# Latent attention: softmax sums by GpSimd and per chunk, two VectorE jobs on ScalarE, maximum read before the copy

## The chip, the cores and the metric

The kernel runs on one NeuronCore of a Trainium2 chip. The metric is the device time of one execution in microseconds (us), and lower is better. TensorE does matrix products into PSUM; VectorE and ScalarE read and write PSUM and SBUF; GpSimd works on SBUF alone. Each engine runs its own instructions in the order of the program and meets the others at semaphores.

## The reference

Two transformer-like layers on x of 2048 tokens by 256. The change touches only the first attention (16 heads, causal, queries and keys of 128 + 64 columns through low-rank latents):

```
q = (_rmsnorm(x @ w_q_a, q_a_ln) @ w_q_b).reshape(b, s, H, DQ)
q_nope, q_pe = (q[..., :DN], q[..., DN:])
ckv = x @ w_kv_a
c_kv, k_pe = (ckv[..., :KL], ckv[..., KL:])
kv = (_rmsnorm(c_kv, kv_a_ln) @ w_kv_b).reshape(b, s, H, DN + DV)
q_pe = _apply_rope(q_pe, cos, sin)
...
scores = jnp.einsum('bqhd,bkhd->bhqk', qf, kf) * scale
scores = jnp.where(mask[None, None], scores, jnp.finfo(scores.dtype).min)
p = jax.nn.softmax(scores, axis=-1)
o = jnp.einsum('bhqk,bkhd->bqhd', p, v).reshape(b, s, H * DV)
return o @ w_out
```

Before it stands a routed FFN; after it a second routed FFN, a mixing FFN, a second attention and another mixing FFN. None of these is touched.

## The kernel before

`latent_heads` does the first attention. Heads go in 8 pairs, and the 2048 queries in 4 chunks of 512 (`CH`), j = 0 to 3. A unit is one head of one chunk, so there are 64 units; the two units of a pair and a chunk stand one behind the other and share a chunk's end (32 of those). Keys go in tiles of 128, and a step is two key tiles: unit j has 2(j+1) steps, the last two of them on the diagonal (tiles of 512, 384, 256 and 128 queries), 320 steps in all. Scores are kept with keys on the partitions and queries along the row.

A step goes through these events:
- `scores`: per key tile three products (high and low parts of query and key) into one of two score buffers in PSUM, used in turn;
- `evac`: ScalarE copies the tile to a slot of `held` in SBUF; `max`: VectorE takes the running maximum per key partition from the same PSUM buffer into `largest`. A score buffer is free for step n + 2 once both are done;
- after the unit's last `max`: `turn_max` (four transposes), `turn_max_out` (VectorE: row maxima, then a diagonal matrix of their negatives, `shift_diag`, L1237 and L1242), `spread` (one product that puts the shift on all partitions);
- some 12 steps behind its scores (`SECOND_PASS_AFTER`): `add` (VectorE adds the shift), `exp` (ScalarE), `values` (TensorE, two 64-column products side by side), and `sum` (GpSimd adds the exponentials of the full tiles into `summed`, L1178 and L1182; diagonal tiles get none);
- per unit `sums` (L1027, L1029): TensorE multiplies `summed` and each diagonal tile, loaded as weights, by one column of ones, 28 instructions for j > 0 and 20 for j = 0; `sums_out` takes the reciprocals (L1283);
- per chunk `widen`, `spread_inverse`, `project`: scaling, and the output projection added to x (L1295).

Each unit's query is made ahead of its scores: `query` (five products), `query_out` (ScalarE copy, L1124), `sine` (VectorE, two 32-partition multiplications with halves exchanged, L1260 and L1261), `cosine`, `whole` (GpSimd, L1188 and L1192), `high` (ScalarE), `low` (GpSimd, L1197).

The order of events on each engine is fixed before the program runs by `latent_plan`: every event has an engine, an estimated duration, a rank and the events it must follow, and a list scheduler walks through them. `HELD_STEPS` (15) is the number of slots of `held`; `evac` of step n waits until step n - 15 has been multiplied and summed. Products outside the score path (`SIDE`) share two PSUM banks in turn.

## Time and profile before

| | us |
|---|---|
| median of 3 runs | 2220.66 |
| lowest, highest | 2203.05, 2222.22 |
| the profiled execution, time | 2205.07 |
| its span, first to last instruction | 2203.3 |
| first attention's heads (`latent_heads`) in it | 146 to 1472, so 1326 |

Over the span TensorE is busy 91%, VectorE 75%, ScalarE 51% and GpSimd 36%, at a mean granted TensorE clock of 0.883. These shares mix stages with different limits. The page of the profile and the trace give times in us, of single instructions in ns; PE is TensorE, PEld its weight loads, DVE VectorE, ACT ScalarE, POOL GpSimd. L1029 is line 1029 of the kernel. The granted clock is a share of full speed, 1.00 for 2.4 GHz and 0.50 for 1.2 GHz. Busy matmuls overlap in the records, so the distance from start to start is the better price of one.

### The profile page before, as it was taken

How to read it: one execution, taken by the hardware profiler on the slowest of the kernel's cores; microseconds unless marked ns; L12 is line 12 of the kernel's file. 1: busy time of each engine (PE TensorE's matmuls, PEld its weight loads, DVE VectorE, ACT ScalarE, POOL GpSimd, SP SyncE). 2: the span in 40 equal slices, each digit the busy share in tenths (PEclk: the TensorE clock that was granted, in tenths of full speed). 3: DMA queues.
4: the chain of work that ended last, by engine and by line, in shares of the span. 5: the costliest groups of instructions: out<-in, count | busy, mean ns of one | idle time of the engine just before them, and what ended most of it. 6: DMA issues, size and time to landing. Idle time of an engine off the chain costs nothing. (4 is left out here: it accounts for less than half of the span.)

```text
span 2203.3 us, 30217 instructions
## 1 busy us (share of the span) xinstructions
PE 2000.7 (91%) x10904; PEld 1238.1 (56%) x10904; DVE 1660.8 (75%) x2525; ACT 1114.9 (51%) x2075; POOL 792.0 (36%) x636
## 2 busy tenths in 40 slices
PE   4769999999999999999999999957497899999996
PEld 3646656657657657566666666636454444444436
DVE  6758887786887796787786887756856788888725
ACT  1235664564564564564564555521032457777771
POOL 0015564563664572573573663430231100000010
PEclk8878998998898998898998898967798779999998
DMA  2200000000000000000000000010233020020001
GB/s 89 69 21 1 1 1 13 1 1 6 8 1 6 9 1 13 1 1 14 1 1 5 1 1 1 1 41 1 71 68 70 2 30 1 1 30 2 2 1 39
DMA packets 26707, 34.53 MB, mean 16 GB/s; under 512 B 5312, under 2 KB 19648, under 8 KB 26432
## 3 DMA queue, kind: packets, MB, share of 16 engines
q1 hardware_dynamic: 25360, 31.28, 6.0%
q8 instruction: 89, 1.46, 0.3%
q10 hardware_dynamic: 1200, 1.31, 0.2%
q14 instruction: 58, 0.48, 0.1%
HBM read 26.03 MB, written 6.29 MB: 15 GB/s over the span
## 5 line engine op out<-in xcount | busy, mean ns | idle before, releaser
L1100 ACT ACTIVATE lath_held<-lath_score 128x512 f32<-128x512 f32 (+1 forms) x448 | 293.5, 686 | 321.3 <-PE lath_score L993 318.7
L1182 POOL TENSOR_TENSOR lath_summed<-lath_summed,lath_held 128x512 f32<-128x512 f32 x288 | 387.5, 1345 | 130.3 <-ACT lath_held L1105 111.7
L1251 DVE TENSOR_TENSOR lath_held<-lath_held,lath_shift 128x512 f32<-128x512 f32 (+1 forms) x448 | 339.5, 792 | 50.5 <-PE lath_shift L1016 49.2
L1895 ACT ACTIVATE atth_probs<-atth_score 128x512 f32<-128x512 f32 (+3 forms) x640 | 293.2, 541 | 153.4 <-PE atth_score L1814 151.1
L1105 ACT ACTIVATE lath_held<-lath_held 128x512 f32<-128x512 f32 (+1 forms) x448 | 306.8, 719 | 116.9 <-DVE lath_held L1251 115.2
L1004 PE MATMUL lath_out<-lath_held,lat_latent 128*64 128x512 f32 (+3 forms) x1280 | 342.3, 599 | 2.4 <-ACT lath_held L1105 2.4
L1854 DVE TENSOR_REDUCE atth_maxima<-atth_slot 128x2 f32<-128x1024 f32 (+3 forms) x288 | 286.0, 1042 | 54.3 <-PE atth_slot L1797 53.3
L989 PE MATMUL lath_score<-lath_query_hi,lat_key_hi 128*128 128x512 f32 (+3 forms) x640 | 281.4, 440 | 10.2 <-DVE lath_largest L1205 7.1
L993 PE MATMUL lath_score<-lath_query_hi,lat_key_lo 128*128 128x512 f32 (+3 forms) x640 | 271.8, 425 | 0.0
L1205 DVE TENSOR_TENSOR lath_largest<-lath_score,lath_largest 128x256 f32<-128x256 f32 (+3 forms) x336 | 222.2, 685 | 62.0 <-ACT lath_held L1100 58.6
L990 PE MATMUL lath_score<-lath_query_lo,lat_key_hi 128*128 128x512 f32 (+3 forms) x640 | 252.4, 394 | 0.0
L989 PEld LDWEIGHTS lath_score<-lath_query_hi,lat_key_hi 128*128 128x128 f32 x640 | 133.6, 209 | 182.1 <-issue 123.7
L1742 POOL TENSOR_SCALAR_AFFINE_SELECT atth_probs<-atth_probs 128x512 f32<-128x512 f32 x64 | 40.8, 637 | 430.8 <-ACT atth_probs L1895 430.8
L1029 PE MATMUL lath_side<-square,lath_held 128*128 128x1 f32 x1280 | 184.1, 260 | 0.5 <-ACT lath_held L1105 0.5
L1029 PEld LDWEIGHTS lath_side<-square,lath_held 128*128 128x128 f32 x1280 | 174.0, 206 | 4.7 <-issue 3.0
L1178 POOL TENSOR_TENSOR lath_summed<-lath_held 128x512 f32<-128x512 f32 x48 | 62.3, 1298 | 307.5 <-ACT lath_held L1105 294.7
L1188 POOL TENSOR_TENSOR lath_turn_a<-lath_query,lat_rope 128x512 f32<-128x512 f32 x64 | 95.5, 1492 | 199.2 <-ACT lath_query L1124 197.8
L1827 PE MATMUL atth_out<-atth_probs,att_v_one 128*32 128x512 f32 (+3 forms) x1280 | 152.1, 549 | 0.6 <-POOL atth_probs L1742 0.5
L993 PEld LDWEIGHTS lath_score<-lath_query_hi,lat_key_lo 128*128 128x128 f32 x640 | 137.6, 215 | 19.9
L990 PEld LDWEIGHTS lath_score<-lath_query_lo,lat_key_hi 128*128 128x128 f32 x640 | 135.4, 212 | 15.8
L1004 PEld LDWEIGHTS lath_out<-lath_held,lat_latent 128*64 128x64 f32 x1280 | 70.4, 144 | 94.0 <-issue 71.6
L1814 PE MATMUL atth_score<-atth_query,att_key 50*128 50x512 f32 (+3 forms) x384 | 116.1, 453 | 1.7 <-ACT atth_probs L1895 1.1
(342 smaller groups left out, 3098.4 us busy)
## 6 DMA issues: line engine op xcount, KB each, us to landing
att_first_query<-att_scratch SPq DMA_DIRECT2D x12, 256.0 KB, 9.0
atth_query<-att_scratch SPq DMA_DIRECT2D x12, 256.0 KB, 8.9
ffn_a_w<-in_L_ffn_W SPq DMA_DIRECT2D x2, 1024.0 KB
lat_raw_out<-in_L_attn_w_out SPq DMA_DIRECT2D x8, 256.0 KB, 2.7
lat_rope<-in_c_rope_feature SPq DMA_DIRECT2D x1, 2048.0 KB, 11.0
ffn_b_w<-in_L_ffn_W SPq DMA_DIRECT2D x2, 1024.0 KB, 7.1
mix_a_factors<-in_L_ffn_factors SPq DMA_DIRECT2D x8, 256.0 KB, 4.0
att_scratch<-attp_high SPq DMA_DIRECT2D x4, 512.0 KB, 2.9
```

Source lines behind the costliest of these rows:

```text
L989: nc.tensor.matmul(scores[:, q0:CH], key_hi[:, keys], hi, start=True, stop=False)
L990: nc.tensor.matmul(scores[:, q0:CH], key_hi[:, keys], lo, start=False, stop=False)
L993: last = nc.tensor.matmul(scores[:, q0:CH], key_lo[:, keys], hi, start=False, stop=True)
L1004: last = nc.tensor.matmul(out_bank[KL * i:KL * i + KL, q0:CH], latent[:, kt, 0:KL], slot(n)[:, i, q0:CH], start=(step == 0), stop=(step == ...
L1029: last = nc.tensor.matmul(bank[:, i:i + 1], slot(end - 2 + d // 2)[:, d % 2, cols], core.ones[:, 0:1], start=(j == 0 and d == 0), stop=(d ...
L1100: nc.scalar.activation(slot(n)[:, tiles, q0:CH], score_bank[n % 2][:, tiles, q0:CH], ACT.Copy)\
L1105: nc.scalar.activation(slot(n)[:, tiles, q0:CH], slot(n)[:, tiles, q0:CH], ACT.Exp, scale=SCALE0)\
L1182: nc.gpsimd.tensor_tensor(total, total, slot(n)[:, i, :], ALU.add).then_inc(s["tiles_summed"], 1)
L1205: nc.vector.tensor_tensor(out, first, second, ALU.max).then_inc(s["maxed"], 1)
L1251: nc.vector.tensor_tensor(slot(n)[:, tiles, q0:CH], slot(n)[:, tiles, q0:CH], shift[:, q0:CH].unsqueeze(1).broadcast_to([P, count, CH - q0 ...
L1854: nc.vector.reduce_max(maxima[:, n % 2, :, pair, i, at], slot[r % 2][:, :, begin:begin + width], AX.X)\
L1895: nc.scalar.activation(probs[:, step % PROB_STEPS, h, q0:CH], score_bank[u % 3][:, q0:CH], ACT.Exp, scale=SCALE1)\
```

## The change

- `sum` now covers the diagonal tiles too: GpSimd adds all four at their own widths (512, 384, 256, 128 queries), for j = 0 as well, beginning there with a zero. `summed` has four buffers in place of two.
- `sums` is done once per chunk. Two products with ones as weights (64 columns each, one head in each half of the bank) give the sums along the row; `sums_out` copies them to SBUF (ScalarE), `turn_sums` turns them with four transposes, and `turn_sums_out` takes all reciprocals at once (VectorE).
- `shift_diag` is made by ScalarE in four copies with a scale per partition (`diag`), no longer by VectorE.
- ScalarE exchanges the halves of the rotated query columns while it copies them from PSUM (two more copies in `query_out`), and VectorE multiplies once on 64 partitions. The sign in the table moves with it.
- `max` waits for the scores alone (at step 1 of a unit for the copy of step 0 too), and `evac` waits for `max`. The scores of step n + 2 wait for `evac` alone.
- `HELD_STEPS` is 14, and the estimates in the plan follow the new work.

```diff
-HELD_STEPS = 15
+HELD_STEPS = 14
@@ sum_parts
-    return 0 if s >= 2 * j else 1 if s == 0 else 2
+    return 1 if s == 0 and LATENT_UNITS[u][1] else 2
@@ tensor
                             pe.wait_ge(s["evacuated"], PARTS_DONE[n - 2])
-                            if MAX_DONE[n - 2]:
-                                pe.wait_ge(s["maxed"], MAX_DONE[n - 2])
...
                     elif kind == "sums":
-                        for i in range(TPC):
-                            cols = slice(i * P, (i + 1) * P)
-                            if j:
-                                nc.tensor.matmul(bank[:, i:i + 1], summed[:, n % 2, cols], core.ones[:, 0:1], start=True, stop=False)
-                            for d in range(i + 1):
-                                last = nc.tensor.matmul(bank[:, i:i + 1], slot(end - 2 + d // 2)[:, d % 2, cols], core.ones[:, 0:1],
-                                                        start=(j == 0 and d == 0), stop=(d == i))
+                        pe.wait_ge(s["tiles_summed"], SUMS_DONE[FIRST_STEP[2 * n + 2] - 1])
+                        for h in range(2):
+                            last = nc.tensor.matmul(bank[KL * h:KL * h + KL, :], core.ones[:, 0:KL], summed[:, (2 * n + h) % 4, :], start=True, stop=True)
+                        last.then_inc(s["side_done"], 1)
+                    elif kind == "turn_sums":
+                        pe.wait_ge(freed(("sums", n)), use["sums", n] // 2 + 1)
                         for i in range(TPC):
+                            last = nc.tensor.transpose(bank[:, i * P:(i + 1) * P], sums_t[:, i * P:(i + 1) * P], core.ident)
@@ scalar
                     if kind == "evac":
                         act.wait_ge(s["scores_done"], n + 1)
+                        if max_parts(n):
+                            act.wait_ge(s["maxed"], MAX_DONE[n] - (1 if j and step == 2 * j + 1 else 0))
...
+                    elif kind == "diag":
+                        act.wait_ge(freed(("turn_max", n)), use["turn_max", n] // 2 + 1)
+                        if n:
+                            act.wait_ge(s["spread_done"], n)
+                        for i in range(TPC):
+                            nc.scalar.activation(shift_diag[:, i], minus_ident[:], ACT.Copy, scale=row_max[:, n % 2, i:i + 1]).then_inc(s["diag_ready"], 1)
+                    elif kind == "sums_out":
+                        wait_side(act, ("sums", n))
+                        nc.scalar.activation(sums_t[:], side(("sums", n))[:], ACT.Copy).then_inc(freed(("sums", n)), 1)
...
                         whole = side(("query", n))
+                        nc.scalar.activation(turn_b[64:96], whole[96:P], ACT.Copy).then_inc(s["halves_swapped"], 1)
+                        nc.scalar.activation(turn_b[96:P], whole[64:96], ACT.Copy).then_inc(s["halves_swapped"], 1)
@@ gpsimd
                         for i in range(2):
+                            q0 = queries_from(2 * step + i, j)
+                            so_far = total[:, q0:CH]
+                            if step == 0 and i == 0:
+                                so_far = zero[:].broadcast_to([P, CH])
+                            else:
+                                pool.wait_ge(s["tiles_summed"], before + i)
+                            nc.gpsimd.tensor_tensor(total[:, q0:CH], so_far, slot(n)[:, i, q0:CH], ALU.add).then_inc(s["tiles_summed"], 1)
@@ vector
                     if kind == "max":
-                        dve.wait_ge(s["evacuated"], PARTS_DONE[n])
+                        dve.wait_ge(s["scores_done"], n + 1)
+                        if step == 1 and j:
+                            dve.wait_ge(s["evacuated"], PARTS_DONE[n - 1])
...
-                        nc.vector.tensor_tensor(shift_diag[:], minus_ident[:].unsqueeze(1).broadcast_to([P, TPC, P]),
-                                                row_max[:].unsqueeze(2).broadcast_to([P, TPC, P]), ALU.mult).then_inc(s["diag_ready"], 1)
...
-                        nc.vector.tensor_tensor(turn_b[64:96], query[96:P, n % 2], rope[96:P, 1, cols], ALU.mult).then_inc(s["sine_done"], 1)
-                        nc.vector.tensor_tensor(turn_b[96:P], query[64:96, n % 2], rope[64:96, 1, cols], ALU.mult).then_inc(s["sine_done"], 1)
+                        dve.wait_ge(s["halves_swapped"], 2 * n + 2)
+                        nc.vector.tensor_tensor(turn_b[64:P], turn_b[64:P], rope[64:P, 1, cols], ALU.mult).then_inc(s["sine_done"], 1)
```

The first place is TensorE at the end of a unit halfway through the stage (the second head of chunk 2 of pair 3, where a chunk ends as well). `lath_score` is a score buffer, `lath_side` a side bank. Before:

```order
L993 MATMUL lath_score0<-lath_query_hi,lat_key_lo 128x512
L1027 MATMUL lath_side0<-square,lath_summed 128x1
L1029 MATMUL lath_side0<-square,lath_held 128x1
L1027 MATMUL lath_side0<-square,lath_summed 128x1
L1029 MATMUL lath_side0<-square,lath_held 128x1 x2
L1027 MATMUL lath_side0<-square,lath_summed 128x1
L1029 MATMUL lath_side0<-square,lath_held 128x1 x3
L1027 MATMUL lath_side0<-square,lath_summed 128x1
L1029 MATMUL lath_side0<-square,lath_held 128x1 x4
L1010 MATMUL lath_side1<-square,lath_largest 128x128 x4
L1004 MATMUL lath_out<-lath_held,lat_latent 64x512 x2
```

and now, at the same chunk's end:

```order
L987 MATMUL lath_score0<-lath_query_hi,lat_key_lo 128x512
L1015 MATMUL lath_side1<-lath_summed,square 64x512 x2
L1004 MATMUL lath_side0<-square,lath_largest 128x128 x4
L998 MATMUL lath_out<-lath_held,lat_latent 64x512 x2
L1020 MATMUL lath_side1<-square,lath_sums_t 128x128 x4
L983 MATMUL lath_score1<-lath_query_hi,lat_key_hi 128x512
```

The 14 one-column products of the unit (each is two instructions in the trace) are gone; the other unit of the chunk has none at all now, and this one has two wide products and four transposes.

The second place is GpSimd over the sums of the first head of chunk 3 of the same pair. Before:

```order
L1178 TENSOR_TENSOR lath_summed<-lath_held 128x512
L1182 TENSOR_TENSOR lath_summed<-lath_summed,lath_held 128x512 x4
L1188 TENSOR_TENSOR lath_turn_a<-lath_query,lat_rope 128x512
L1182 TENSOR_TENSOR lath_summed<-lath_summed,lath_held 128x512 x6
L1197 TENSOR_TENSOR lath_query_lo<-lath_query,lath_query_hi 128x512
```

and now:

```order
L1183 TENSOR_TENSOR lath_summed<-lath_held 128x512
L1192 TENSOR_TENSOR lath_summed<-lath_summed,lath_held 128x512 x4
L1198 TENSOR_TENSOR lath_turn_a<-lath_query,lat_rope 128x512
L1192 TENSOR_TENSOR lath_summed<-lath_summed,lath_held 128x512 x4
L1202 TENSOR_TENSOR lath_query<-lath_turn_a,lath_turn_b 128x512
L1207 TENSOR_TENSOR lath_query_lo<-lath_query,lath_query_hi 128x512
L1192 TENSOR_TENSOR lath_summed<-lath_summed,lath_held 128x512 x3
L1192 TENSOR_TENSOR lath_summed<-lath_summed,lath_held 128x384
L1192 TENSOR_TENSOR lath_summed<-lath_summed,lath_held 128x256
L1192 TENSOR_TENSOR lath_summed<-lath_summed,lath_held 128x128
```

The unit's sum now ends with its four diagonal tiles, and the jobs of the next queries stand between them and behind them.

## Rows read from the trace of the kernel before

**Rows 1.** Windows view, the stage: us; busy PE, PEld, DVE, ACT, POOL; granted clock; DMA share.

```profile
146.00:1472.00 1326.00, 1289.14 (x6297) 831.17 (x6296) 1031.37 (x1408) 727.48 (x1216) 711.67 (x528) 0.89 0.02 5
```

**Rows 2.** Groups by line and form, TensorE: the sums' one-column products.

```profile
L1029 PE MATMUL lath_side<-square,lath_held 128*128 128x1 f32 x1280 | 184.1, 260 | 0.5 <-ACT lath_held L1105 0.5
...
L1027 PE MATMUL lath_side<-square,lath_summed 128*128 128x1 f32 x384 | 68.6, 248 | 10.6 <-POOL lath_summed L1182 7.6 <-DVE x L1295 1.6 <-ACT lath_held L1105 1.4
```

**Rows 3.** Timeline, TensorE: start us, us, instructions merged.

```profile
1085.81 1.03 PE L1004 MATMUL lath_out<-lath_held,lat_latent 128*64 128x512 f32 x4
...
1086.76 0.50 PE L989 MATMUL lath_score<-lath_query_hi,lat_key_hi 128*128 128x512 f32 x1
...
1088.26 0.28 PE L1027 MATMUL lath_side<-square,lath_summed 128*128 128x1 f32 x2
...
1090.41 1.03 PE L1029 MATMUL lath_side<-square,lath_held 128*128 128x1 f32 x8
...
1091.31 0.63 PE L1010 MATMUL lath_side<-square,lath_largest 128*128 128x128 f32 x4
...
1145.54 0.66 PE L1010 MATMUL lath_side<-square,lath_largest 128*128 128x128 f32 x4
```

**Rows 4.** Windows view, TensorE: us, busy (count), granted clock, DMA share, GB/s.

```profile
1090.00:1092.00 2.00, 2.00 (x19) 1.00 0.00 0
...
1092.00:1094.00 2.00, 2.00 (x6) 0.62 0.00 0
...
1096.00:1098.00 2.00, 2.00 (x9) 1.00 0.00 0
...
1147.00:1150.00 3.00, 3.00 (x16) 1.00 0.00 0
```

**Rows 5.** Waits, TensorE: score products (total us, times, longest).

```profile
PE lath_score L989 <- DVE lath_largest L1205: 7.1, 13, 1.1
```

**Rows 6.** Groups by line and form, GpSimd.

```profile
L1182 POOL TENSOR_TENSOR lath_summed<-lath_summed,lath_held 128x512 f32<-128x512 f32 x288 | 387.5, 1345 | 130.3 <-ACT lath_held L1105 111.7
...
L1197 POOL TENSOR_TENSOR lath_query_lo<-lath_query,lath_query_hi 128x512 fp32r<-128x512 f32 x64 | 89.7, 1402 | 54.3 <-ACT lath_query_hi L1129 54.3
...
L1192 POOL TENSOR_TENSOR lath_query<-lath_turn_a,lath_turn_b 128x512 f32<-128x512 f32 x64 | 82.2, 1284 | 54.2 <-DVE lath_turn_b L1261 53.2 <-PE lath_side L1029 0.7
...
L1588 POOL TENSOR_TENSOR attp_turned<-attp_by_cos,attp_by_sin 128x256 f32<-128x256 f32 x16 | 13.6, 848 | 50.4 <-DVE attp_by_sin L1563 50.4
```

**Rows 7.** Groups by line and form, VectorE.

```profile
L1261 DVE TENSOR_TENSOR lath_turn_b<-lath_query,lat_rope 32x512 f32<-32x512 f32 x64 | 78.8, 1232 | 2.0
...
L1260 DVE TENSOR_TENSOR lath_turn_b<-lath_query,lat_rope 32x512 f32<-32x512 f32 x64 | 71.4, 1115 | 10.4 <-ACT lath_query L1124 7.0 <-POOL lath_query L1192 1.5
...
L1205 DVE TENSOR_TENSOR lath_largest<-lath_score,lath_largest 128x1024 f32<-128x1024 f32 x96 | 117.1, 1219 | 30.7 <-ACT lath_held L1100 29.9
...
L1242 DVE TENSOR_TENSOR lath_shift_diag<-lath_minus_ident,lath_row_max 128x512 fp32r<-128x512 f32 x64 | 55.3, 865 | 2.2
```

**Rows 8.** Timeline, VectorE and GpSimd: a sine pair.

```profile
1304.77 0.69 DVE L1260 TENSOR_TENSOR lath_turn_b<-lath_query,lat_rope 32x512 f32<-32x512 f32 x1
...
1305.48 1.66 DVE L1261 TENSOR_TENSOR lath_turn_b<-lath_query,lat_rope 32x512 f32<-32x512 f32 x1
...
1304.78 1.81 POOL L1197 TENSOR_TENSOR lath_query_lo<-lath_query,lath_query_hi 128x512 fp32r<-128x512 f32 x1
```

**Rows 9.** Groups by line and form, ScalarE.

```profile
L1100 ACT ACTIVATE lath_held<-lath_score 128x1024 f32<-128x1024 f32 x192 | 196.0, 1021 | 198.3 <-PE lath_score L993 196.3
...
L1113 ACT ACTIVATE lath_half<-lath_out 64x512 f32<-64x512 f32 x48 | 28.6, 596 | 19.8 <-PE lath_out L1004 18.9
...
L1105 ACT ACTIVATE lath_held<-lath_held 128x128 f32<-128x128 f32 x64 | 19.4, 303 | 0.0
```

**Rows 10.** Timeline, the stage's end: last GpSimd sums, last residual add.

```profile
1444.07 13.67 POOL L1182 TENSOR_TENSOR lath_summed<-lath_summed,lath_held 128x512 f32<-128x512 f32 x10
...
1470.77 0.69 DVE L1295 TENSOR_TENSOR x<-lath_side,x 128x512 f32<-128x512 f32 x1 [1.01 <-PE lath_side L1044]
```

More of the change, by code:

```diff
@@ L732 @@
 PER_PAIR = 2 * NCH
-HELD_STEPS = 15
+HELD_STEPS = 14
 SECOND_PASS_AFTER = 12.0
 QUERY_SLOTS = 3
-SIDE = ("turn_q", "turn_kv", "fold_query", "fold_out", "query", "turn_max", "sums", "spread_inverse", "project")
+SIDE = ("turn_q", "turn_kv", "fold_query", "fold_out", "query", "turn_max", "sums", "turn_sums", "spread_inverse", "project")
 def step_parts(g):
@@ L810, in latent_plan @@
         k, due, last = NCH * p + j, FIRST_STEP[u] - 6.0, FIRST_STEP[u + 1] - 1
-        add("tensor", 1.3, due, ("query", u), ("split_low", p), of("low", u - 2))
-        add("scalar", 0.55, due, ("query_out", u), ("query", u))
-        add("vector", 1.2, due, ("sine", u), ("query_out", u), of("whole", u - 1))
+        add("tensor", 1.3, due, ("query", u), ("split_low", p), of("low", u - 2), of("whole", u - 1))
+        add("scalar", 1.5, due, ("query_out", u), ("query", u))
+        add("vector", 0.9, due, ("sine", u), ("query_out", u))
         add("pool", 1.3, due, ("cosine", u), ("query_out", u), of("whole", u - 1))
@@ L838, in latent_plan @@
         held = g - HELD_STEPS
-        add("tensor", 0.1 + 3 * total / 2250, g, ("scores", g), ("low", u), of("scores", g - 1), of("evac", g - 2), of("max", g - 2))
-        full = s < 2 * j
-        if held < 0:
-            summed = None
-        elif LATENT_STEPS[held][1] < 2 * LATENT_UNITS[LATENT_STEPS[held][0]][1]:
-            summed = ("sum", held)
-        else:
-            summed = ("sums", LATENT_STEPS[held][0])
-        add("scalar", on_scalar, g, ("evac", g), ("scores", g), of("values", held), summed)
-        add("vector", 0.0 if j and s == 0 else elementwise + (0.6 if j and s == 2 * j + 1 else 0.0), g + 1.0, ("max", g), ("evac", g),
-            of("max", g - 1), of("turn_max", u - 2) if s == 0 else None)
-        add("vector", elementwise, late - 1.0, ("add", g), ("spread", u), ("max", g), of("add", g - 1))
+        add("tensor", 0.1 + 3 * total / 2250, g, ("scores", g), ("low", u), of("scores", g - 1), of("evac", g - 2))
+        add("scalar", on_scalar, g, ("evac", g), ("max", g), of("values", held), of("sum", held))
+        add("vector", 0.0 if j and s == 0 else elementwise + (0.6 if j and s == 2 * j + 1 else 0.0), g, ("max", g), ("scores", g), of("evac", g - 1), of("max", g - 1),
+             of("turn_max", u - 2) if s == 0 else None)
+        add("vector", elementwise, late - 1.0, ("add", g), ("spread", u), ("evac", g), of("add", g - 1))
         add("scalar", on_scalar, late - 0.6, ("exp", g), ("add", g), of("exp", g - 1))
@@ L853, in latent_plan @@
             of("fold", u - 1) if s == 0 else None)
-        if full:
-            add("pool", sum_parts(g) * 1.3, late, ("sum", g), ("exp", g), ("sum", g - 1) if s else None, of("sums", u - 2) if s == 0 else None)
+        add("pool", (1.3 if sum_parts(g) == 1 else sum(0.15 + w / 420 for w in widths) if len(widths) > 1 else 2.6), late, ("sum", g), ("exp", g), of("sum", g - 1),
+            of("sums", u // 2 - 2) if s == 0 else None)
     followers, missing = {}, {}
@@ L1114, in _ @@
                     elif kind == "widen":
-                        for u in (2 * n, 2 * n + 1):
-                            act.wait_ge(freed(("sums", u)), use["sums", u] // 2 + 1)
+                        act.wait_ge(freed(("turn_sums", n)), use["turn_sums", n] // 2 + 1)
                         if n:
@@ L1172, in _ @@
                         _, j, _ = LATENT_UNITS[u]
[L1173 removed]
+                        total, before = summed[:, u % 4], SUMS_DONE[n] - sum_parts(n)
                         pool.wait_ge(s["exp_done"], PARTS_DONE[n])
[L1175 to L1177 removed]
+                        if step == 0 and u >= 4:
+                            wait_side(pool, ("sums", u // 2 - 2))
+                        if step == 0 and j:
                             nc.gpsimd.tensor_tensor(total, slot(n)[:, 0, :], slot(n)[:, 1, :], ALU.add).then_inc(s["tiles_summed"], 1)
```

77 lines of the change are left out of this document (35 added, 42 removed).

## The prediction

> **What bounds the kernel now.** I read the windows view first, since the change touches one stage only. From 146 to 1472 us, 1326 us of the span, TensorE is busy 1289, VectorE 1031, ScalarE 727 and GpSimd 712 [rows 1]. So TensorE sets the pace of this stage and every other engine has slack. The waits confirm it: over 320 steps the score products waited 7.1 us for VectorE's maximum [rows 5]. What TensorE spends its time on is the groups view, and there the one-column products for the softmax sums stand out: 1280 and 384 instructions, 184.1 and 68.6 us busy, for results four columns wide [rows 2]. The timeline gives their real price, since busy times overlap: the 28 instructions of one unit begin at 1088.26 and the next work at 1091.31, so 3.05 us, or 0.109 us each [rows 3]. The third view is the granted clock. It stands at 1.00 (2.4 GHz) while such a run goes by, falls to 0.62 of full speed on average in the window behind it (part of it at 0.50, 1.2 GHz), and is back at 1.00 by 1096 [rows 4]. What TensorE did right before the fall was this run of one-column products. Over the stage the mean is 0.89 [rows 1].
>
> **The change, part by part.** Everything is a sum against the profiled execution, 2205.07 us, with the stage's 1326 us as the part that moves.
>
> *Sums on TensorE.* The 1664 one-column instructions go: 1664 x 0.109 = 181 us at the full clock. New are, per chunk, two products of 512 columns in the two halves of a bank, in form like a step of `values`, which took 0.95 us from 1085.81 to the next start at 1086.76, and four transposes like `turn_max`, 0.63 us [rows 3]. 32 x 1.58 = 51 us. Net -130.
>
> *The clock.* A mean of 0.89 between two levels of 0.5 and 1 says that 22% of the stage, 292 us, ran at 1.2 GHz. If the cause is the one-column runs and they are gone, the same work takes 146 us less. That is the other half of the gain, and it takes no cover from anywhere: -146. Bounds: nothing if another cause cools the clock, -146 if none does. I take the whole, because the rows beside a lone `turn_max` (1145.54, four transposes as in the new code) show the window after it at 1.00 [rows 3, 4]. TensorE's own floor for the stage is then 1326 - 130 - 146 = 1050 us.
>
> *Sums on GpSimd.* It gets four more additions per unit, 1280 columns. In proportion to the 512-column addition of 1.345 us that is 3.36 us; the 256-column row with 0.848 us says that short ones cost more than their share, and a straight line through the two gives 0.35 us each plus the columns, 3.88 us [rows 6]. 64 units: 215 to 248, I take 232. GpSimd's work becomes 712 + 232 = 944 us. It is no longer the idle engine, and its queue has waits that more slack doesn't remove: 54.3 us for ScalarE's high part and 54.2 us for VectorE's sine, with the query chain of three jobs going to and fro [rows 6]. I keep both, 108. At the start of the stage it has nothing for about 9 us plus some 15 us of ramp before exponentials exist (an estimate), and behind its last sum at 1457.7 the stage goes on for 14 us to 1471.5 [rows 10]. 944 + 108 + 24 + 14 = 1090 us. **GpSimd becomes the bound**, 40 us above TensorE.
>
> *VectorE.* `shift_diag` goes (55.3), the two sine jobs of 1.12 and 1.23 us become one [rows 7]. The new one has the same number of columns on 64 partitions; an undisturbed one took 0.69 and one beside a GpSimd job 1.66 [rows 8], so 44 to 106 us against 150 before; I take 75. VectorE: 1031 - 55 - 75 = about 900 us (870 to 932), off the bound.
>
> *ScalarE.* Four 128-column copies per unit, by the 303 ns row 78 us; two half copies from PSUM per query, 128 at the 0.596 us of a copy of 64 partitions, 76 us; 32 copies of sums, 19 us [rows 9]. 727 + 173 = 900 us, off the bound, with a longer queue.
>
> *Order of maximum and copy.* The score buffer is freed by the same two jobs in the other sequence: 1.22 (maximum) and 1.02 (copy) [rows 7, 9]. No gain on that chain: 0 by itself. What it moves is who waits: ScalarE's copy now stands in its queue until VectorE is done, and behind it are exponentials (for which TensorE's values and GpSimd's sums wait), query copies and the new diagonal copies. Cover: exponentials run some steps ahead of the values that need them. If the cover fails it costs TensorE a part of a step each time; that is the second rival. One slot of `held` less tightens the same loop, since a copy waits for the sum of 14 steps before: 12 steps of lag leave GpSimd two steps, some 5 us, to be late in.
>
> *Tail and constants.* The last unit's four extra additions, 3.4 to 3.9 us, stand behind 13.67 us of its sums [rows 10]; the shorter product run behind them gives about that back. One more memset and a sign in a table: nothing.
>
> **The sum.** GpSimd's 1090, plus 20 us for slips, since TensorE stood idle 37 us in the stage even when it alone was short [rows 1] and four engines will now be at 80% or more. Stage 1110, so 216 us less: 2205 - 216 = 1989. The profiled execution was 15.6 us below the median of the runs shown; the scatter between 2203 and 2222 is most likely the machine's, and I give the new kernel two thirds of it: **2000 us**.
>
> *Where the skill speaks against it.* GpSimd and VectorE get in each other's way in this trace: at 1304.77 a sine job ran its 0.69 us while the GpSimd job that began with it took 1.81, against its group's mean of 1.40, and the next sine job took 1.66 [rows 6, 8]. The Trainium skill, GPSIMD Engine Reference, Specifications, says that GpSimd's SBUF interfaces are shared with VectorE, with contention when VectorE has two SBUF inputs; by that rule, the trace agrees, a fuller GpSimd meets more such jobs. But the change also takes away one sine job and the diagonal per unit, 128 of 240 such jobs. Were every one of the 112 that remain to cost GpSimd those 0.4 us, it would be 45 us on its 1090, within the second rival.
>
> **Rivals.**
>
> *TensorE keeps the pace.* GpSimd's 108 us of waits were slack that closes when it is busy, its sums slide past them, and the stage ends near TensorE's 1050 to 1070: 2205 - 266 + 11 = 1950. For it: the waits of rows 6 were measured on an idle engine. Against it: four engines at 85 to 95%.
>
> *Lockstep.* All four engines wait for each other a little in queues of fixed order, because the estimates by which the order was laid down differ from the true durations (in the plan GpSimd's low part stands at 1.3 us and ScalarE's wide copy at 0.95, against 1.40 and 1.02 measured [rows 6, 9]). Taken as 0.25 to 0.5 us of new TensorE wait per step, 320 steps give 80 to 160 us over the floor of 1050, to which new idle time might add a colder clock: stage 1150 to 1230, 2040 to 2120. For it: the balance above. Against it: before, with VectorE at 78%, TensorE lost almost nothing.
>
> *The clock still falls.* If transposes and idle time cool it as the one-column products did, each chunk's new pair and four transposes next to `turn_max` bring one cold stretch as long as one behind each of the 64 runs before, 292 / 64 = 4.6 us, half of it lost: 32 x 2.3 = 74 us on top, about 2075. Against it: the window behind the lone transposes [rows 4]. The Trainium skill, TensorE: Matmul & The Clock Gate, Part 4, says that transposes don't count as busy for the clock gate; by that rule this rival would come true, and the lone `turn_max` speaks against it here.
>
> *Slower.* The place is the score buffer. For two steps the loop is one set of scores (1.50 us [rows 3]), maximum 1.22, copy 1.02 and some 0.6 us of hand-overs, 4.3 us, against TensorE's own 2 x 2.45 = 4.9 us at full clock. It fits with 0.6 us to spare. If at each turn a shift addition (1.2) stands ahead of the maximum and an exponential (1.05) ahead of the copy, the loop is 6.6 us and TensorE waits 0.85 us per step; 320 x 0.86 = 276 us eats the whole gain, and from there on the kernel is slower; with a clock that cools in those waits, about 2250. For it: ScalarE's queue is now behind VectorE's. Against it: the same two jobs in the other sequence were in this loop before, and TensorE waited 7.1 us in all [rows 5].
>
> **How the numbers follow.** GpSimd's pace 0.52 (1975 to 2030), TensorE's pace 0.13 (1935 to 1975), lockstep 0.25 (2030 to 2120), clock 0.04 (2050 to 2090), slower 0.04, no change within 1% 0.02. The range leaves out the lower end of the TensorE case and the upper ends of lockstep and slower: 1942 to 2105. A measurement of this kernel can tell about 1% from no change. Faster by over 1%: 0.94; within: 0.02; slower: 0.04.
>
> **What would show it.** In the profile after: a granted clock of 0.97 or more over the stage, with no fall behind the chunk sums (the clock term); GpSimd busy 930 to 960 us there and rarely idle except in the query chain; TensorE busy below 95% of the stage, its waits naming ScalarE's copies or, at the chunk's sums, GpSimd; VectorE and ScalarE each near 900 us. Wrong would be: a mean clock at 0.9 still; short GpSimd additions well over 1 us each; score products that wait for the copy through the whole of chunk 3; or GpSimd's waits shrinking to a few us, which leaves TensorE's pace and a time under 1960.

## The result, and the profile after

The changed kernel takes 2015.72 us (median; 2009.53 to 2020.40) against 2220.65 us (2203.05 to 2222.22), a ratio of 0.9086 with a 95% interval of 0.9039 to 0.9133. Its profiled execution took 2015.19 us.

The windows view of the first attention's stage, with the columns of [rows 1] (us; busy PE, PEld, DVE, ACT, POOL; granted clock; DMA share):

```profile
141.00:1267.00 1126.00, 1053.63 (x4896) 611.67 (x4896) 886.50 (x1254) 883.67 (x1633) 923.52 (x784) 0.97 0.02 5
```

The stage has gone from 1329 us (142 to 1471; the 1326 of [rows 1] begin 4 us later) to 1126. TensorE is busy 1054 us, 235 less than in [rows 1], and its clock is 0.97 in place of 0.89. GpSimd has 924 us, VectorE 887, ScalarE 884. Of these 203 us the execution keeps some 190: from the stage's end to the end of the span it is 746 us now and was 732, in code that the change doesn't touch (experiment 8 comes back to this).

What answers to [rows 2] is one group of 128 instructions (count, busy us and mean ns, idle before) in place of 1664:

```profile
L1015 PE MATMUL lath_side<-lath_summed,square 128*64 128x512 f32 x128 | 38.7, 663 | 19.3 <-POOL lath_summed L1192 18.2 <-ACT lath_query L1129 0.9
```

On TensorE's timeline a chunk's end looks like this, as [rows 3] did for a unit's:

```profile
902.09 1.08 PE L1015 MATMUL lath_side<-lath_summed,square 128*64 128x512 f32 x4
...
902.97 1.08 PE L998 MATMUL lath_out<-lath_held,lat_latent 128*64 128x512 f32 x4
...
903.98 0.66 PE L1020 MATMUL lath_side<-square,lath_sums_t 128*128 128x128 f32 x4
...
904.39 0.48 PE L983 MATMUL lath_score<-lath_query_hi,lat_key_hi 128*128 128x512 f32 x1
```

The pair of wide products takes 0.88 us to the next start (902.09 to 902.97), the four transposes 0.41 (903.98 to 904.39). And against [rows 4] the clock now falls nowhere behind the sums of a chunk. Inside the stage it falls at the start of a pair of heads, six times; the rest of its time at 1.2 GHz stands in the stage's first 40 us and in its tail. One of the six (windows of 4 us, TensorE busy, granted clock):

```profile
728.00:732.00 4.00, 1.94 (x11) 1.00 0.00 0
...
732.00:736.00 4.00, 3.08 (x8) 0.64 0.01 2
...
736.00:740.00 4.00, 4.00 (x13) 0.51 0.00 0
...
740.00:744.00 4.00, 4.00 (x23) 1.00 0.00 0
```

TensorE was busy for 1.94 of 4 us with the clock at 1.00, and then it is 0.64 and 0.51. Here it stood idle before the fall, and in the 4 us before each of the other five it was busy for 1.73 to 2.04 us. Before the change it fell right behind one-column products with TensorE busy all the time: of its 52 falls between 170 and 1440 us, 51 have such products in the 4 us ahead of them. TensorE's waits (total us, times, longest), beside [rows 5]:

```profile
PE lath_score L983 <- ACT lath_held L1090: 21.2, 31, 1.7
...
PE lath_side L1015 <- POOL lath_summed L1192: 18.2, 10, 10.6
...
PE lath_out L998 <- ACT lath_held L1095: 5.6, 4, 3.0
```

They are short and of several kinds. Together with the rest the stage has 72 us in which TensorE is idle, 37 before.

GpSimd's groups, beside [rows 6]:

```profile
L1192 POOL TENSOR_TENSOR lath_summed<-lath_summed,lath_held 128x512 f32<-128x512 f32 x336 | 443.7, 1321 | 31.3 <-ACT lath_held L1095 6.6 <-POOL lath_summed L1183 0.4
...
L1192 POOL TENSOR_TENSOR lath_summed<-lath_summed,lath_held 128x256 f32<-128x256 f32 x64 | 49.7, 776 | 5.2
...
L1192 POOL TENSOR_TENSOR lath_summed<-lath_summed,lath_held 128x128 f32<-128x128 f32 x64 | 32.7, 511 | 5.0
...
L1207 POOL TENSOR_TENSOR lath_query_lo<-lath_query,lath_query_hi 128x512 fp32r<-128x512 f32 x64 | 84.7, 1323 | 9.3 <-ACT lath_query_hi L1134 9.3
...
L1202 POOL TENSOR_TENSOR lath_query<-lath_turn_a,lath_turn_b 128x512 f32<-128x512 f32 x64 | 84.8, 1325 | 4.7 <-DVE lath_turn_b L1269 3.5
```

The 512-column addition costs what it did. The short ones, 776 and 511 ns, are dearer than their share of columns. And the two waits of the query chain, 54.3 and 54.2 us before, are 9.3 and 4.7. GpSimd's largest wait in the stage is another, for the exponentials at a unit's first sum:

```profile
POOL lath_summed L1183 <- ACT lath_held L1095: 89.8, 23, 8.5
```

The new sine job of VectorE and the new copies of ScalarE, beside [rows 7, 9]:

```profile
L1269 DVE TENSOR_TENSOR lath_turn_b<-lath_turn_b,lat_rope 64x512 f32<-64x512 f32 x64 | 65.8, 1028 | 30.6 <-ACT lath_turn_b L1128 21.7 <-PE lath_score L987 7.7
```

```profile
L1102 ACT ACTIVATE lath_shift_diag<-lath_minus_ident,lath_row_max 128x128 fp32r<-128x128 f32 x256 | 81.6, 393 | 19.5 <-DVE lath_row_max L1252 19.2
...
L1127 ACT ACTIVATE lath_turn_b<-lath_side 32x512 f32<-32x512 f32 x64 | 37.8, 591 | 16.7 <-PE lath_side L1043 15.5
```

At the stage's end, beside [rows 10]:

```profile
1240.07 16.17 POOL L1192 TENSOR_TENSOR lath_summed<-lath_summed,lath_held 128x512 f32<-128x512 f32 x13
...
1256.38 1.98 PE L1015 MATMUL lath_side<-lath_summed,square 128*64 128x512 f32 x4 [10.58 <-POOL lath_summed L1192]
...
1266.98 0.69 DVE L1303 TENSOR_TENSOR x<-lath_side,x 128x512 f32<-128x512 f32 x1 [1.02 <-PE lath_side L1034]
```

GpSimd's last sums run for 16.17 us and end at 1256.24; only then can TensorE start the last chunk's products, and the stage ends 11.4 us later.

### The profile page after: what moved, and what is told of

It is laid out like the page before. It is cut to its first block and busy times, and to the rows that moved or that the text cites. A ratio compares the mean times of both kernels' runs of the same rounds, so it can differ in the third digit from the quotient of the medians.

```text
span 2013.2 us, 28359 instructions
## 1 busy us (share of the span) xinstructions
PE 1776.6 (88%) x9496; PEld 1022.7 (51%) x9496; DVE 1515.9 (75%) x2366; ACT 1271.1 (63%) x2491; POOL 1003.5 (50%) x892
## 5 line engine op out<-in xcount | busy, mean ns | idle before, releaser
L1192 POOL TENSOR_TENSOR lath_summed<-lath_summed,lath_held 128x512 f32<-128x512 f32 (+3 forms) x528 | 595.7, 1128 | 46.5 <-ACT lath_held L1095 6.6
L998 PE MATMUL lath_out<-lath_held,lat_latent 128*64 128x512 f32 (+3 forms) x1280 | 312.7, 553 | 6.4 <-ACT lath_held L1095 5.6
L983 PE MATMUL lath_score<-lath_query_hi,lat_key_hi 128*128 128x512 f32 (+3 forms) x640 | 261.8, 409 | 23.0 <-ACT lath_held L1090 21.2
L987 PE MATMUL lath_score<-lath_query_hi,lat_key_lo 128*128 128x512 f32 (+3 forms) x640 | 255.9, 400 | 0.0
L984 PE MATMUL lath_score<-lath_query_lo,lat_key_hi 128*128 128x512 f32 (+3 forms) x640 | 237.6, 371 | 0.0
L983 PEld LDWEIGHTS lath_score<-lath_query_hi,lat_key_hi 128*128 128x128 f32 x640 | 123.1, 192 | 157.5 <-issue 98.5
L987 PEld LDWEIGHTS lath_score<-lath_query_hi,lat_key_lo 128*128 128x128 f32 x640 | 126.5, 198 | 17.5
L984 PEld LDWEIGHTS lath_score<-lath_query_lo,lat_key_hi 128*128 128x128 f32 x640 | 123.5, 193 | 14.5
L1183 POOL TENSOR_TENSOR lath_summed<-lath_held 128x512 f32<-128x512 f32 x48 | 61.8, 1287 | 89.9 <-ACT lath_held L1095 89.8
L1822 PEld LDWEIGHTS atth_score<-atth_query,att_key 50*128 50x128 f32 x384 | 52.3, 189 | 90.7 <-ACT atth_probs L1903 82.6
L1215 DVE TENSOR_TENSOR lath_largest<-lath_score,lath_held 128x1024 f32<-128x1024 f32 x48 | 58.7, 1224 | 50.5 <-PE lath_score L987 31.7
```

What stands on the lines that cost most here:

```text
L983: nc.tensor.matmul(scores[:, q0:CH], key_hi[:, keys], hi, start=True, stop=False)
L984: nc.tensor.matmul(scores[:, q0:CH], key_hi[:, keys], lo, start=False, stop=False)
L987: last = nc.tensor.matmul(scores[:, q0:CH], key_lo[:, keys], hi, start=False, stop=True)
L998: last = nc.tensor.matmul(out_bank[KL * i:KL * i + KL, q0:CH], latent[:, kt, 0:KL], slot(n)[:, i, q0:CH], start=(step == 0), stop=(step == ...
L1192: nc.gpsimd.tensor_tensor(total[:, q0:CH], so_far, slot(n)[:, i, q0:CH], ALU.add).then_inc(s["tiles_summed"], 1)
L1215: nc.vector.tensor_tensor(out, first, second, ALU.max).then_inc(s["maxed"], 1)
```

## Experiments

All times are medians with the ratio to the kernel before, timed together with it on the same chip. Stage times are from the first to the last instruction of `latent_heads` in each profile, one execution each; the kernel before, profiled twice, shows 1330 and 1335 us, so differences of about 5 us between stages say nothing.

**1. wide_ones: the one-column products 128 columns wide.** The kernel before, same instructions and same order; the other 127 columns are copies of the sum.

```diff
-nc.tensor.matmul(bank[:, i:i + 1], summed[:, n % 2, cols], core.ones[:, 0:1], ...)
+nc.tensor.matmul(bank[:, cols], summed[:, n % 2, cols], core.ones, ...)
```

> The kernel before, with its sum products multiplied by 128 columns of ones in place of one (same instruction count, same sums in column 0 of each block of 128). Theory A, the few columns of these runs cool TensorE's clock: the granted clock of the first attention's heads rises from 0.89 to 0.97 or more, the stage goes from 1326 to 1190-1230 us and the time to 2070-2110 us. Theory B, the clock falls for another reason at a unit's end (idle time, the transposes): the clock stays at 0.89 and the time within 1% of 2205-2220 us.

Measured: 2110.82 us, ratio 0.9571 (0.9518 to 0.9624). The stage:

```profile
141.00:1364.00 1223.00, 1181.87 (x6304) 766.13 (x6304) 1030.94 (x1412) 727.25 (x1217) 714.69 (x528) 0.98 0.02 5
```

A unit's 28 instructions still take 3.1 us on the timeline, as in [rows 3]:

```profile
1012.36 0.39 PE L1027 MATMUL lath_side<-square,lath_summed 128*128 128x128 f32 x2
...
1015.49 0.60 PE L1010 MATMUL lath_side<-square,lath_largest 128*128 128x128 f32 x4
```

and behind them the clock stays where it was (windows of 2 us):

```profile
1014.00:1016.00 2.00, 2.00 (x19) 1.00 0.04 8
...
1016.00:1018.00 2.00, 2.00 (x9) 1.00 0.00 0
```

So the runs of one-column products were what TensorE did when its clock fell, and 106 of the 1329 us hung on it: theory A, with 106 us where 146 were put down. VectorE, ScalarE and GpSimd had the same work in the same order, so nothing else moved. The clock alone is about half of what the change brings.

**2. one_product: one product per unit in place of its sums.** It leaves the softmax sums out.

```diff
-for i in range(TPC): ... one-column products over summed and the diagonal tiles
+last = nc.tensor.matmul(bank[:, 0:TPC], slot(end - 2)[:, 0, 0:P], core.ones[:, 0:TPC], start=True, stop=True)
```

> The kernel before with one product per unit in place of the 20 to 28 instructions of its sums; it leaves out the softmax sums, so the output isn't scaled rightly. Theory A (one-column products cost 181 us by themselves and 146 by the clock): TensorE alone would need 1000 us for the stage, but VectorE's 1031 us of work is then the longest, so the stage is 1060-1110 and the time 1940-1990 us, the clock 0.97 or more. Theory B (the clock falls for another reason): stage 1145 or more, time 2025-2050 us at a clock of 0.89.

Measured: 2018.76 us, ratio 0.9166 (0.9120 to 0.9213). The stage, and TensorE's largest wait in it:

```profile
141.00:1280.00 1139.00, 1031.47 (x4768) 601.07 (x4768) 1028.16 (x1413) 724.57 (x1217) 714.81 (x528) 0.97 0.02 5
```

```profile
PE lath_score L989 <- DVE lath_largest L1199: 26.6, 37, 2.3
```

The clock is 0.97, as theory A has it, but the stage is 1139 us and not the 1060 to 1110 expected: with TensorE at 1031 and VectorE at 1028 us of work neither is near full, and the score products wait for the maximum nearly four times as long as before. This kernel has none of the change's new work, and VectorE has all of its old work; it ends 13 us above the changed one. So with the sums simply gone from TensorE the stage meets a limit elsewhere. What the new sums themselves cost is read against sums_alone (experiment 5), with the same order of copy and maximum and the same work on VectorE: 256 us more on GpSimd and 31 more on TensorE make that stage 24 us longer, 1163 for 1139 us.

**3. short_diag: GpSimd's diagonal additions cut to 4 columns.** It leaves those parts out of the sums. The first addition of a unit of chunk 0 keeps its 512 columns, and the order of events is that of the changed kernel.

```diff
-q0 = queries_from(2 * step + i, j)
+q0 = queries_from(2 * step + i, j) if step < 2 * j else CH - 4
```

> The changed kernel with GpSimd's additions of the diagonal tiles cut to 4 columns each (it leaves those parts of the sums out); GpSimd's load falls from 924 to about 730 us. Theory of the prediction, GpSimd sets the pace: the stage falls by 100 us or more, time 1870-1915 us. Rival, TensorE still sets it and waits for GpSimd only at the chunk sums and at the tail (18.2 us of waits): 10-25 us less, 1990-2005 us.

Measured: 2002.30 us, ratio 0.9099 (0.9056 to 0.9141), not to be told from the changed kernel's 0.9086.

```profile
144.00:1256.00 1112.00, 1045.82 (x4896) 603.99 (x4896) 882.33 (x1252) 882.77 (x1633) 764.73 (x784) 0.98 0.02 5
```

159 us less work for GpSimd, 14 us less stage, and a time inside the rival's 1990 to 2005 us. GpSimd doesn't set the pace; the prediction's first theory falls. And with more slack on GpSimd the two waits of the query chain are back, from 9.3 and 4.7 us to 50.1 and 14.1:

```profile
L1207 POOL TENSOR_TENSOR lath_query_lo<-lath_query,lath_query_hi 128x512 fp32r<-128x512 f32 x64 | 85.1, 1329 | 50.1 <-ACT lath_query_hi L1134 50.0
...
L1202 POOL TENSOR_TENSOR lath_query<-lath_turn_a,lath_turn_b 128x512 f32<-128x512 f32 x64 | 82.5, 1290 | 14.1 <-DVE lath_turn_b L1269 13.0
```

**4. light_tensor: one of three products per score tile less.** It leaves out the key's high part by the query's low part.

```diff
-nc.tensor.matmul(scores[:, q0:CH], key_hi[:, keys], lo, start=False, stop=False)
```

> The changed kernel without one of the three products of each score tile (high part of the key by low part of the query; the scores lose precision), 640 products of about 0.2 us or 128 us of TensorE's 1054. Theory A, TensorE sets the pace of the changed stage: 100-128 us less, 1890-1915 us. Theory B, lockstep of four engines at 80% and more: the others (GpSimd 924, VectorE 887, ScalarE 884 us) hold the stage at 1060-1100, so 30-65 us less, 1950-1985 us.

Measured: 1993.44 us, ratio 0.8997 (0.8962 to 0.9032).

```profile
141.00:1244.00 1103.00, 950.83 (x4256) 510.88 (x4256) 884.55 (x1253) 882.56 (x1633) 922.62 (x784) 0.95 0.02 5
```

```profile
PE lath_score L983 <- ACT lath_held L1089: 47.2, 58, 1.9
...
PE lath_side L1014 <- POOL lath_summed L1191: 46.5, 24, 11.0
```

103 us less work for TensorE, 23 us less stage. TensorE's waits for ScalarE's copy more than double, and those for GpSimd's sums too. So TensorE doesn't set the pace alone either; the gain is smaller even than theory B expected. Two reservations: the plan's estimates still hold the third product, and another order might make more of it; and the stage has 114 us at 1.2 GHz here, 79 in the changed kernel (mean clock 0.95 for 0.97), which takes back a part of the gain.

**5. sums_alone, order_back, moves_back: the change taken apart.** In order_back the copy goes first again, in moves_back VectorE makes the diagonal matrix and both sine products again, sums_alone has both.

```diff
 # order_back
-dve.wait_ge(s["scores_done"], n + 1)
+dve.wait_ge(s["evacuated"], PARTS_DONE[n])
-act.wait_ge(s["maxed"], MAX_DONE[n] - (1 if j and step == 2 * j + 1 else 0))
+pe.wait_ge(s["maxed"], MAX_DONE[n - 2])
 # moves_back
-for i in range(TPC):
-    nc.scalar.activation(shift_diag[:, i], minus_ident[:], ACT.Copy, scale=row_max[:, n % 2, i:i + 1])
+nc.vector.tensor_tensor(shift_diag[:], minus_ident[:]..., row_max[:, n % 2]..., ALU.mult)
-nc.vector.tensor_tensor(turn_b[64:P], turn_b[64:P], rope[64:P, 1, cols], ALU.mult)
+nc.vector.tensor_tensor(turn_b[64:96], query[96:P, n % 2], rope[96:P, 1, cols], ALU.mult)
+nc.vector.tensor_tensor(turn_b[96:P], query[64:96, n % 2], rope[64:96, 1, cols], ALU.mult)
```

> The changed kernel with the order of maximum and copy as before and with the diagonal matrix and the exchanged halves back on VectorE: of the change only the sums remain. VectorE has 1025 us of work again, ScalarE 750, GpSimd 925. Theory A, the sums carry nearly all of the gain and VectorE fits beside: 2020-2045 us. Theory B, VectorE's 1025 us become the bound once TensorE's floor is 1050: stage 1180-1230, time 2070-2120 us, and the two other parts are worth 50 us or more.

> The changed kernel with the order of maximum and copy as before: the copy waits for the scores alone, the maximum for the copy, the next scores for both. Theory A, the order by itself is worth nothing and only moves who waits: within 0.5% of the changed kernel, 2005-2025 us. Theory B, maximum first frees VectorE earlier at each step and carries part of the 40 us that the stage loses when both other parts are taken back: 2030-2050 us.

> The changed kernel with the diagonal matrix and the exchanged halves back on VectorE (busy 1025 us of the stage instead of 887), maximum first. Theory A, VectorE's load is what costs the 40 us: 2040-2055 us, with TensorE's score products waiting for the maximum or the copy behind it. Theory B, the order carries it: 2010-2025 us.

Measured: sums_alone 2046.51 us, 0.9289 (0.9244 to 0.9334); order_back 2014.55 us, 0.9110 (0.9085 to 0.9135); moves_back 2069.53 us, 0.9347 (0.9322 to 0.9373). Their stages, in that order:

```profile
144.00:1307.00 1163.00, 1062.35 (x4896) 612.02 (x4896) 1031.90 (x1380) 740.16 (x1249) 971.08 (x784) 0.96 0.02 5
```

```profile
144.00:1274.00 1130.00, 1050.63 (x4896) 602.75 (x4896) 906.66 (x1253) 882.37 (x1633) 923.94 (x784) 0.97 0.02 5
```

```profile
144.00:1328.00 1184.00, 1069.34 (x4896) 612.86 (x4896) 1036.75 (x1381) 742.51 (x1249) 965.38 (x784) 0.96 0.02 5
```

The stage of sums_alone is 37 us longer than the changed one's, and its time lies 1.5 us above the range of its theory A. The order by itself is worth nothing (1130 for 1126 us): theory A. It only moves who waits: TensorE's score products wait 16.0 us for the maximum in order_back, 21.2 for the copy in the changed kernel. moves_back is slower than either of its theories had it (2055 us at most). The two moves are worth 33 us with the copy first (1163 to 1130) and 58 with the maximum first (1184 to 1126). With VectorE at 1037 us of work, maximum first looks like the worse order, by 21 us in these profiles and 0.6% in the ratios; but the ratios' intervals overlap, so this isn't shown.

**6. diag_back and sine_back: one move taken back at a time.** The edits are the two halves of moves_back.

> The changed kernel with only the diagonal matrix back on VectorE (one job of 0.87 us per unit in place of four copies of 0.32; VectorE about 940 us, ScalarE 800). moves_back cost 54 us with both. Theory A, it is VectorE's load that costs, in proportion: 55 of 138 us come back, so 15-25 us, 2030-2040 us. Theory B, its place does: the job stands in the chain between row maxima and shift, so its share is larger than its load: 2045 us or more.

> The changed kernel with only the exchanged halves back in VectorE's two sine jobs (VectorE about 970 us, ScalarE 808). Theory A, load in proportion: 30-40 us, 2045-2055 us. Theory B, place: the sine is far ahead of its use, so it costs less than its load, 2020-2035 us.

Measured: diag_back 2042.38 us, 0.9220 (0.9191 to 0.9248); sine_back 2050.12 us, 0.9244 (0.9212 to 0.9275).

```profile
142.00:1303.00 1161.00, 1065.94 (x4896) 609.31 (x4896) 951.25 (x1318) 815.37 (x1377) 941.25 (x784) 0.97 0.02 5
```

```profile
143.00:1304.00 1161.00, 1067.28 (x4896) 604.70 (x4896) 984.31 (x1317) 815.40 (x1505) 944.77 (x784) 0.96 0.02 5
```

The diagonal matrix brings VectorE 65 us and the stage 35, the sine 98 us and also 35. In both ScalarE has 68 us less. The time of diag_back lies between its two theories, that of sine_back in its theory A. Per microsecond moved the diagonal matrix costs more than the sine in the stages (0.54 against 0.36), which would speak for its place in the chain between row maxima and shift. By the ratios, 0.9220 and 0.9244 for 0.9086, it is 30 and 35 us, so 0.46 against 0.36, and the intervals of the two overlap; the difference isn't shown. What both say together: a microsecond put on VectorE cost this stage a third to a half, even when ScalarE is relieved by the same edit; one taken from TensorE gave 0.22 (experiment 4), one from GpSimd 0.09 (experiment 3).

The comparison has a gap. short_diag and light_tensor run the order of events of the changed kernel; moving a job changes the plan, and in experiments 5 and 6 all four engines go through their events in another order. Experiment 7 has a kernel in which another order of the same work cost 21 us of stage. All four kernels with work put back on VectorE are slower, by 35 to 58 us, but how much of that is load and how much order these runs don't separate.

**7. replan and lag_11: the same work in another order.**

```diff
 # replan
-add("scalar", 1.5, due, ("query_out", u), ("query", u))
+add("scalar", 1.8, due, ("query_out", u), ("query", u))
-on_scalar = sum(0.1 + w / 1200 for w in widths)
+on_scalar = sum(0.18 + w / 1200 for w in widths)
... (six more estimates likewise)
 # lag_11
-SECOND_PASS_AFTER = 12.0
+SECOND_PASS_AFTER = 11.0
```

> The changed kernel with the estimates of its plan set to the durations measured in its own trace (query copies 1.8 us for 1.5, the diagonal matrix 1.3 for 1.2, cosine 1.45 for 1.3, sine 1.05 for 0.9, wide copy 1.03 for 0.95); the work is the same, only the order moves. Theory A, the 73 us that TensorE stands idle in the stage come from a plan that is off: 15-40 us less, 1975-2000 us. Theory B, they come from loops between engines at 80% that no order cures: within 10 us of 2015.

> The changed kernel with the second pass ranked 11 steps behind the scores in place of 12, so that GpSimd's sums have three steps until their slot is needed. Theory A, the 14 slots bind (copies wait for sums of 14 steps before): 5-20 us less. Theory B, they don't, since exponentials in fact run 6 to 8 steps behind: within 0.5% of 2015 us.

Measured: replan 2034.95 us, 0.9182 (0.9149 to 0.9214); lag_11 2013.63 us, 0.9085 (0.9057 to 0.9113).

```profile
142.00:1289.00 1147.00, 1053.86 (x4896) 608.54 (x4896) 887.88 (x1253) 887.90 (x1633) 924.79 (x784) 0.97 0.02 5
```

```profile
142.00:1267.00 1125.00, 1049.27 (x4896) 608.91 (x4896) 888.83 (x1254) 885.55 (x1633) 925.11 (x784) 0.97 0.02 5
```

lag_11 is the changed kernel within the interval: the 14 slots don't bind (in the changed kernel ScalarE's copies waited 0.7 us in all for GpSimd's sums). replan is slower by about 1%, with the same work and truer estimates. Its profiled execution took 2051 us, 16 above its median, but 759 of them lie behind the stage, 746 in the changed kernel; the 21 us that its stage is longer answer to the 19 between the medians. Neither theory holds as written: order does matter at this balance, but truer estimates don't find the better one.

**8. before_again: the kernel before, profiled a second time.** No edit.

> The kernel before, unchanged, for a second profile. In the changed kernel's profile the untouched second attention took 474 us against 459 in the profile of before, with 113 us of its time at 1.2 GHz against 79, and in four variants 470 to 471 us with 106. Theory A, this differs from execution to execution: the second profile of the same kernel shows another value, 465-475 us. Theory B, it belongs to the program: 459 us again.

Measured: 2224.18 us in its one execution. TensorE in the second attention, untouched by all of this (us, busy and count, granted clock), in the first profile of before, in this one and in the changed kernel's:

```profile
1685.00:2144.00 459.00, 438.45 (x2896) 0.92 0.09 12
```

```profile
1692.00:2166.00 474.00, 453.35 (x2896) 0.88 0.09 11
```

```profile
1482.00:1956.00 474.00, 452.96 (x2896) 0.89 0.09 11
```

2896 instructions each time, and 459, 474 and 474 us at clocks of 0.92, 0.88 and 0.89. Theory A: it differs from execution to execution. The 15 us that the first comparison seems to lose there are none of the change; from the stage's end to the end of the span this execution has 746 us, as the changed kernel has.

## Why the prediction was right

The time lies in the range and 16 us from the number. The gain and its two sources on TensorE were seen rightly. What would hold the new stage was not, and that the number came so near is luck. By its steps:

- **What bounds the kernel**: right, TensorE, with the one-column products as its dispensable part. one_product and wide_ones show it from two sides.
- **Sums on TensorE, -130**: TensorE's busy time fell by 235 us in all, and wide_ones puts the clock's part of that at 107 (1289 to 1182); 128 are left for the work. The pair and the transposes took 1.29 us where shown, not 1.58, which makes it 140 by the prices; the difference lies in the clock, since the changed stage has more time at 1.2 GHz than wide_ones (79 us, 39).
- **The clock, -146**: the cause is shown; the size was too large. The step took half of all time at 1.2 GHz as saved. wide_ones gained 106 us while the stage's time at 1.2 GHz went from 292 us to 39 (mean clock 0.89 and 0.98), so the lower clock cost 0.42 of the time spent in it and not 0.5, and some of that time stays: 79 us in the changed stage.
- **TensorE's floor, 1050**: its busy time is 1054, which is partly luck. The sum began at the stage's 1326 us with 37 us of idle time in them. From the busy time it is 1289 - 276 = 1013, and 39 of the 41 us that are missing are the clock's (107 for 146).
- **Sums on GpSimd, 232 more**: 924 in place of 712, 212 more. The straight line through two rows was the better shape (511 and 776 ns for 128 and 256 columns, 0.60 and 0.85 us put down), while other jobs of GpSimd became a little shorter.
- **GpSimd becomes the bound**: this is the step that failed. It rested on keeping 108 us of waits in the query chain as a cost, and those fell to 14; in short_diag, where GpSimd has more slack, they are 64 again, so they come and go with its slack. The 89.8 us for which GpSimd waits for exponentials at the units' first sums weren't in the sum. Nor does GpSimd bind: short_diag took 159 us off it for 14. With the waits at 14 the prediction's own sum is 944 + 14 + 24 + 14 = 996 us, below TensorE's 1050, and its sign of being wrong (waits of a few us, TensorE's pace, a time under 1960) came true in the waits and not in the time. What held the stage at 1126 fits the second rival, lockstep, in a milder form than its 1150 to 1230: taking 103 us from TensorE gave 23, taking work from GpSimd almost nothing, and the kernels with work put back on VectorE lost a third to a half of it. That 1110 came out near 1126 is luck: the 60 us over TensorE's 1050 that were put down to GpSimd stand where 76 us with another cause were measured.
- **VectorE and ScalarE, 900 each**: 887 and 884. The sine job took 1.03 us, inside its bounds, the two half copies 0.59 each; the diagonal copies have 82 us of busy time for the 78 put down (0.39 us each, but four in a row overlap). The sine job of 0.69 us in [rows 8] was called undisturbed and had a GpSimd job beside it; in the whole trace of before the 30 sine jobs without one took 0.69 us too, the others 1.16 (first half) and 1.56 (second half) on average.
- **"Off the bound"** for VectorE isn't borne out: sums_alone, moves_back, diag_back and sine_back, with 951 to 1037 us on it, have stages 35 to 58 us longer. They are also ordered otherwise, so this is a strong hint and no proof that its work weighs most.
- **Order of maximum and copy, 0**: right (order_back). **One slot less, possibly tight**: it isn't (lag_11).
- **The clock still falls** was the right rival to give little: no fall stands behind the transposes of `turn_max` and the new ones where they are shown, nor behind 128-column products in the place of the old ones. The falls that are left stand behind or among idle time: 27 us at 1.2 GHz at six pair starts, some 29 in the stage's first 40 us and 23 in its tail, 79 in all (a mean of 0.97 over 1126 us).
- **Slower**: the loop over the score buffer held, TensorE's wait there is 21.2 us. Its 0.6 us of hand-overs came from no row; one of them, from the end of a copy to the next scores, took 0.14 us (732.13 to 732.27, shown below). And 320 x 0.85 is 272 us and not 276, which changes nothing.

The places where TensorE waits at a pair's start can be read on ScalarE's timeline:

```profile
723.61 1.00 ACT L1090 ACTIVATE lath_held<-lath_score 128x1024 f32<-128x1024 f32 x1
...
724.64 0.59 ACT L1114 ACTIVATE lath_half<-lath_out 64x512 f32<-64x512 f32 x1
...
725.14 0.62 ACT L1134 ACTIVATE lath_query_hi<-lath_query 128x512 fp32r<-128x512 f32 x1
...
727.01 0.60 ACT L1129 ACTIVATE lath_query<-lath_side 128x512 f32<-128x512 f32 x1
...
727.50 1.02 ACT L1090 ACTIVATE lath_held<-lath_score 128x1024 f32<-128x1024 f32 x1
...
728.41 1.27 ACT L1102 ACTIVATE lath_shift_diag<-lath_minus_ident,lath_row_max 128x128 fp32r<-128x128 f32 x4
...
731.15 0.98 ACT L1090 ACTIVATE lath_held<-lath_score 128x512 f32<-128x512 f32 x2
```

From 724.64 to 727.50 it works off a half, a high part and the three query copies, and only then copies scores, which lets TensorE's scores of 728.57 begin. Behind that copy stand a diagonal matrix, another half and two exponentials; the next score copy begins at 731.15, and the scores that need its buffer at 732.27:

```profile
732.27 0.47 PE L983 MATMUL lath_score<-lath_query_hi,lat_key_hi 128*128 128x512 f32 x1 [1.60 <-ACT lath_held L1090]
```

What stays open: whether taking work from VectorE in the changed kernel pays as much as giving it costs, how much of that cost is the changed order, and which loop carries it. No kernel here changes the load of VectorE, or that of ScalarE alone, with the order held. The tail, where 11 us of waiting for GpSimd's last sums are in plain view, wasn't tried either. No kernel here is faster than the changed one and computes all of it; light_tensor is 1% faster and leaves a product out.

## What to carry to other kernels

Price a run of tiny products twice: by its own time, and by the granted clock in the stretch behind it; widening the free dimension of such products is a one-line test of the second. When removing work from the bounding engine brings the others to 80%, don't count on a next single bound: give each engine a weight by taking away or adding a known amount of its work, with the order of events held, since the busiest by share need not be the one that costs. And waits that an idle engine shows in the profile before are no forecast of its waits when its queue is full.

## What the runs showed of the hardware

- A run of 28 one-column products with TensorE busy throughout was followed by a stretch at 1.2 GHz [rows 3, 4]; the same run with 128 columns, 3.13 against 3.05 us long, was not (stage clock 0.98 against 0.89). The width from 1 to 128 columns cost 0.08 us for the whole run.
- The untouched second attention took 459 us in one profile of the kernel before and 474 in the other, along with its granted clock, 0.92 and 0.88. That is as much as some differences between the variants here, and it is why stage times and ratios are read side by side.
- GpSimd's addition took 511, 776 and 1321 ns for 128, 256 and 512 columns, which is some 0.24 us for each instruction beside 2.1 ns a column.
- ScalarE's copy of 128 columns with a scale per partition took 393 ns from start to end, against 280 ns for its plain copy of 128 columns from PSUM and 307 ns for an exponential of 128 columns. Four in a row overlap: 256 of them have 81.6 us of busy time, 0.32 us each.
